# A triangular inversion of 62 small operations goes from VectorE's queue to GpSimd's, with an earlier turn

## What is computed

```python
logits = einsum('bhqd,bhkd->bhqk', q, k) * scale        # 16 heads of 8
probs = softmax(logits + causal_mask)
L = eye(s) - tril(probs, -1)
rhs = diagonal(probs)[..., None] * v
A = solve_triangular(L, rhs, lower=True)
x = x + ga * (A.transpose(0, 2, 1, 3).reshape(b, s, HID) @ Wd.T + bd)
```

## Time and profile before

| | us |
|---|---|
| median of 3 runs | 2507.65 (2505.02 to 2507.76) |
| the profiled execution | 2516.91 |
| its span, first to last instruction | 2515.2 |
| PE busy | 1845.2 (73%) |
| DVE busy | 1649.4 (66%), 3581 instructions |
| ACT busy | 548.0 (22%) |
| POOL busy | 466.2 (19%), 170 instructions |
| PE's granted clock, mean | 0.66 of full speed |

### The profile page before, as it was taken

One profiled execution on the slowest core, in us unless ns is written; L12 is line 12 of the kernel. 1 busy time (PEld: TensorE's weight loads), 2 busy tenths in 40 slices (PEclk: granted clock), 3 DMA queues, 4 the chain that ended last, 5 costly groups with the idle time before them and its releaser, 6 DMA issues.

```text
span 2515.2 us, 47927 instructions
## 1 busy us (share of the span) xinstructions
PE 1845.2 (73%) x20840; PEld 1331.0 (53%) x20840; DVE 1649.4 (66%) x3581; ACT 548.0 (22%) x787; POOL 466.2 (19%) x170
## 2 busy tenths in 40 slices
PE   1566436667677777777876976887888888888869
PEld 1343324444445444444543654666676767675759
DVE  6564367778866877678678547575656666657574
ACT  1100111222222323333333431111112120202010
POOL 9000011111110101001001100313131404040313
PEclk8666555555555556556557656696969696868687
DMA  3042942222111221012021120000000000000000
GB/s 118 2 99 64 151 96 50 50 50 50 46 36 26 49 50 44 8 49 44 8 44 43 40 73 1 1 5 1 5 1 5 1 5 1 5 1 5 1 5 5
DMA packets 130210, 83.87 MB, mean 33 GB/s; under 512 B 100690, under 2 KB 118100, under 8 KB 125524
## 3 DMA queue, kind: packets, MB, share of 16 engines
q1 hardware_dynamic: 130004, 80.85, 14.5%
HBM read 31.54 MB, written 49.28 MB: 32 GB/s over the span
## 4 chain that ended last, share of the span: by engine, by line
PE 44%; DVE 36%; issue 12%; POOL 2%; SPq 2%; DMA 2%; ACT 1%; DVEq 0%; POOLq 0%; ACTq 0%
PE pb L967 11%; DVE mraw L1159 8%; DVE zb L1207 6%; DVE tb L1202 6%; PE pb L975 5%; PE pb L954 4%; PE pb L850 3%; PE pb L801 2%; PE pb L762 2%; PE pb L870 2%; PE pb L880 1%; POOL cst L537 1%; DVE iv L1270 1%; DVE h L1247 1%; PE pb L946 1%
## 5 line engine op out<-in xcount | busy, mean ns | idle before, releaser
L1159 DVE TENSOR_REDUCE mraw<-pb 128x2 f32<-128x1024 f32 (+3 forms) x304 | 354.3, 1165 | 167.5 <-PE pb L806 123.2
L967 PE MATMUL pb<-r,hoty 128*128 128x64 f32 x2048 | 339.7, 348 | 75.4 <-DVE su L1335 45.3
L563 POOL TENSOR_TENSOR r<-hotx,wbd 128x2048 f32<-128x2048 f32 x32 | 248.7, 7771 | 753.8 <-DVE hotx L1322 753.8
L967 PEld LDWEIGHTS pb<-r,hoty 128*128 128x128 f32 x2048 | 336.5, 262 | 79.6 <-DVE su L1335 46.6
L801 PE MATMUL pb<-kall,qa 48*128 48x512 bf16 (+3 forms) x768 | 166.8, 473 | 244.9 <-DVE mraw L1159 193.2
L616 ACT ACTIVATE et<-pb 128x1024 f32<-128x1024 f32 x224 | 229.0, 1024 | 310.5 <-PE pb L817 309.3
L1202 DVE TENSOR_TENSOR tb<-cst,zb 128x31 f32<-128x31 f32 (+15 forms) x496 | 194.2, 392 | 65.8 <-POOL cst L537 53.2
L1207 DVE TENSOR_TENSOR zb<-zb,tb 128x31 f32<-128x31 f32 (+15 forms) x496 | 201.0, 405 | 13.5
L850 PE MATMUL pb<-et,a_all 128*9 128x128 f32 x3584 | 204.7, 368 | 1.7 <-ACT et L616 1.2
L1335 DVE TENSOR_TENSOR su<-su,pb 128x512 f32<-128x512 f32 x128 | 87.2, 686 | 176.1 <-PE pb L967 176.1
L801 PEld LDWEIGHTS pb<-kall,qa 48*128 48x128 bf16 x768 | 38.0, 110 | 306.7 <-DVE mraw L1159 243.7
(11 more groups left out here) (174 smaller groups left out, 2443.8 us busy)
## 6 DMA issues: line engine op xcount, KB each, us to landing
ed_d<-ed SPq DMA_DIRECT2D x32, 1024.0 KB, 4.6
cst<-ed_d SPq DMA_DIRECT2D x128, 64.0 KB, 5.1
qs_d<-qkp SPq DMA_DIRECT2D x48, 128.0 KB, 2.2
ks_d<-qkp SPq DMA_DIRECT2D x48, 128.0 KB, 2.3
qa<-qs_d SPq DMA_DIRECT2D x64, 96.0 KB, 2.6
kall<-ks_d SPq DMA_DIRECT2D x8, 672.0 KB, 21.2
xin<-L_attn_hidden_states SPq DMA_DIRECT2D x4, 512.0 KB
out<-xs SPq DMA_DIRECT2D x8, 256.0 KB, 2.2
```

The costliest lines, as they stand in the source:

```text
L563: nc.gpsimd.tensor_tensor(r4[:, n_ % 2, :, :, :], hotx[:, n_ % 2, :, :].unsqueeze(2).broadcast_to([P, NT, P // NT, NCH]), wbd[:, t, :, :]. ...
L967: last = mm(spread_w(q)[:, j].rearrange("p g c -> p (g c)"), hoty[:, n % 2, at, :], r4[:, n % 2, at, :, :].rearrange("p g c -> p (g c)"), ...
L1159: V.reduce_max(mraw[:, bb, :, g0:g0 + count, c0 // 512], pb[0][:, :].rearrange("p (e n) -> p e n", e=2)[:, :, 0:count * w].rearrange("p e ...
```

## The change

The 62 operations of an inversion leave DVE's queue for POOL's. There inversion s - 1 is cut in three around the masks of step s: 15 pairs of operations (blocks 0 to 2) or 2(2i - 1) pairs before mask (s, 0), three pairs between the masks, and the rest behind mask (s, 1). That makes 10, 14, 18, 22 and 26 pairs ahead of the masks for blocks 3 to 7. The last inversion stands behind all steps. DVE's plan keeps its begin and its turn, with one quota of 4 for all blocks from 3 on, so that the turn is 15 slots behind the begin: the begins of ss = 8 and 9 move to slots 150 and 170, and the solve groups of ss = 7 to 14 begin at slots 147, 167, 187, 211, 235, 263, 291 and 323. The turn waits for POOL's semaphore `inv_done`, in DVE's queue in front of the maxima of that slot. Behind the list the turn of the last inversion stands between two pairs of gates.

```diff
--- before.py
+++ after.py
@@ -108,7 +108,7 @@
             "e_lg", "exp_done", "av_done", "ed_masked", "ed_st0", "ed_st1", "x_ld0", "x_ld1",
             "r_done", "rT_sb", "rn_ps", "r_evac",
 
-            "rd_ready", "rdb_ready", "xb_ready", "zb_ready", "pool_link", "rn_ready", "z_ready", "px_done", "acur", "acc_done", "rr_ready",
+            "rd_ready", "rdb_ready", "xb_ready", "inv_done", "pool_link", "rn_ready", "z_ready", "px_done", "acur", "acc_done", "rr_ready",
 
             "xa_ld", "xr_ld", "tab_ld",
             "ac_ready", "at_ps", "at_sb", "y_ps", "h2_ready", "var2", "sd2", "h2T_ps", "h2T_sb", "gu_ps", "sg", "act",
@@ -362,7 +362,7 @@
                 room = first[ss + 1] + len(chunks_of(ss + 1)) - at
                 quota = -(-NOPS // room)
             else:
-                quota = 3 if block_of(ss + 1) > 3 else 4
+                quota = 4
             left = NOPS
             while left:
                 inv_at[at] = (ss, min(quota, left))
@@ -522,7 +522,7 @@
                 if ss:
                     g.wait_ge(s["z_ready"], ss)
                 lk(nc.gpsimd.memset(zb[:, :, :], 0.0))
-                nc.gpsimd.memset(zb[:, :, :].rearrange("p k i -> p (k i)")[:, 0:NB * NB:NB + 1], 1.0).then_inc(s["zb_ready"], 1)
+                lk(nc.gpsimd.memset(zb[:, :, :].rearrange("p k i -> p (k i)")[:, 0:NB * NB:NB + 1], 1.0))
 
             def mask(s_, bb):
                 wait_alone(g, "exp_done", chunk(s_, bb, 1) + 1, "passed_pool")
@@ -535,6 +535,21 @@
                 g.wait_ge(s["rdb_ready"], ss + 1)
                 g.wait_ge(s[x_ld[par]], 16 * 2 * NC * (ss // 2 + 1))
                 nc.gpsimd.tensor_tensor(xb[:, par, :, :], xb[:, par, :, :], rdb[:, :].unsqueeze(1).broadcast_to([P, NB, NB]), ALU.mult).then_inc(s["xb_ready"], 1)
+                g.wait_ge(s["xb_ready"], ss + 1)
+
+            def inverse(ss):
+
+                par = ss % 2
+                for j in range(NB - 1):
+                    w, u = NB - 1 - j, j + 1
+                    lk(nc.gpsimd.tensor_tensor(tb[:, 0:u, 0:w], xb[:, par, j:j + 1, u:].broadcast_to([P, u, w]),
+                                               zb[:, 0:u, j:j + 1].broadcast_to([P, u, w]), ALU.mult))
+                    total = nc.gpsimd.tensor_tensor(zb[:, 0:u, u:], zb[:, 0:u, u:], tb[:, 0:u, 0:w], ALU.add)
+                    if j < NB - 2:
+                        lk(total)
+                    else:
+                        total.then_inc(s["inv_done"], 1)
+                    yield
 
             def right_side(ss):
                 i, pr, par = block_of(ss), ss % 2, ss % 2
@@ -548,12 +563,26 @@
                 g.wait_ge(s["rd_ready"], ss + 1)
                 nc.gpsimd.tensor_tensor(to, to, rdn[:, par, :].rearrange("p (b h) -> p b h", b=2).unsqueeze(3).broadcast_to([P, 2, H, HD]), ALU.mult).then_inc(s["rn_ready"], 1)
 
+            def steps_of(work, count):
+                for _ in range(count):
+                    next(work, None)
+
             for s_ in range(STEPS):
-                mask(s_, 0)
-                mask(s_, 1)
+                if s_:
+                    i = block_of(s_)
+                    work = inverse(s_ - 1)
+                    steps_of(work, 15 if i <= 2 else (2 * i - 1) * 2)
+                    mask(s_, 0)
+                    steps_of(work, 3)
+                    mask(s_, 1)
+                    run(work)
+                else:
+                    mask(s_, 0)
+                    mask(s_, 1)
                 clear_inverse(s_)
                 scaled(s_)
                 right_side(s_)
+            run(inverse(STEPS - 1))
             for i in range(NI):
                 for t in range(B):
                     n_ = B * i + t
@@ -1191,25 +1220,8 @@
                 v.wait_ge(s["dve"], n[0])
                 v.sem_inc(s["rdb_ready"], 1)
 
-            def inverse(ss):
-
-                par = ss % 2
-                v.wait_ge(s["zb_ready"], ss + 1)
-                v.wait_ge(s["xb_ready"], ss + 1)
-                for j in range(NB - 1):
-                    w, u = NB - 1 - j, j + 1
-                    v.wait_ge(s["dve"], n[0])
-                    V.tensor_tensor(tb[:, 0:u, 0:w], xb[:, par, j:j + 1, u:].broadcast_to([P, u, w]),
-                                    zb[:, 0:u, j:j + 1].broadcast_to([P, u, w]), ALU.mult).then_inc(s["dve"], 1)
-                    n[0] += 1
-                    yield
-                    v.wait_ge(s["dve"], n[0])
-                    V.tensor_tensor(zb[:, 0:u, u:], zb[:, 0:u, u:], tb[:, 0:u, 0:w], ALU.add).then_inc(s["dve"], 1)
-                    n[0] += 1
-                    yield
-
             def turn_inverse(ss):
-                v.wait_ge(s["dve"], n[0])
+                v.wait_ge(s["inv_done"], ss + 1)
                 if ss:
                     v.wait_ge(s["px_done"], 4 * ss)
                 V.transpose(vt[:, :, :].rearrange("p m i -> p i m"), zb[:, :, :].rearrange("p k i -> p i k")).then_inc(s["z_ready"], 1)
@@ -1250,8 +1262,8 @@
                 lk(V.tensor_tensor(h2[:, :, :], h2[:, :, :], mod[:, :, 4, :], ALU.mult))
                 V.tensor_tensor(h2[:, :, :], h2[:, :, :], mod[:, :, 3, :], ALU.add).then_inc(s["h2_ready"], 1)
 
-            def gates(i):
-                for c in range(4):
+            def gates(i, cs=range(4)):
+                for c in cs:
                     v.wait_ge(s["sg"], 4 * i + c + 1)
                     V.tensor_tensor(hid[:, c, :, :].rearrange("p b n -> p (b n)"), sg[:, c % 2, :], pair(c)[:, 512:1024], ALU.mult).then_inc(s["act"], 1)
 
@@ -1343,19 +1355,13 @@
             nothing = iter(())
             for k in prologue:
                 max_job(k, nothing)
-            work = nothing
             for g_ in range(LAST):
-                if g_ in begin_at:
-                    work = inverse(begin_at[g_])
-
                 def some(g_=g_):
                     if g_ in begin_at:
                         begin_inverse(begin_at[g_])
                     if g_ in inv_at:
                         ss, count = inv_at[g_]
-                        for _ in range(count):
-                            next(work)
-                            yield
+                        yield
                         if inv_at.get(g_ + 1, (None, 0))[0] != ss:
                             turn_inverse(ss)
                 for k in jobs_at[2 * g_]:
@@ -1373,9 +1379,9 @@
             begin_inverse(STEPS - 1)
             attention_out(0)
             normed(0)
-            run(inverse(STEPS - 1))
+            gates(0, (0, 1))
             turn_inverse(STEPS - 1)
-            gates(0)
+            gates(0, (2, 3))
             next_rows(STEPS - 1, 1)
             keys_left = best_keys(0)
             next(keys_left)
```

## The result

The changed kernel takes 2549.56 us (median of 4, 2546.59 to 2554.18) against 2507.7 for the kernel before in the same measurement: ratio 1.0162, interval 1.0132 to 1.0192. Forecast were 2496 us. The profiled execution took 2548.56 us around a span of 2546.8, so the two profiled spans differ by 31.6 us. The medians differ by 41.9, since the profiled execution of the kernel before was 9.3 us above its median; what follows accounts for the 31.6.

The account below looks back on a forecast made before the run. The inversion's two operations held 24.3% of the attention stage's chain, with VectorE the bound early and TensorE close behind later. Terms -3 + 14 - 47 + 19 + 1 + 4 = -12 us took 2507.65 to 2496 us; range 2436 to 2562.

Parts of the forecast that it names:

- Three regimes: Attention stage: VectorE bounds inversions 0 to 3, TensorE is about as busy in 7 to 11, no maxima are left in 14.
- What one inversion costs on POOL: 62 operations on POOL, priced from operations of 256 and 1024 elements: 34 us, bounds 31 and 50 us.
- The link: Between an operation on POOL and its linked successor: 0.08 us from end to start.
- Steps 0 to 4: First five steps: 44.8 us each from begin to turn on POOL, what lies behind the turn unchanged; -3 us.
- Step 5: 18 pairs wait for slot 105's exponentials, which a mask of step 6 needs: 64 us against the window's 50.4, +13.7 us.
- Steps 6 to 13: Turn 15 slots behind the begin instead of 20, solve groups spread out, POOL's path 46.8 us in late steps: -47 us.
- The price of a plain slot behind the turn: Each of the five plain slots that now fall behind the turn, with no solve group or inversion: 2.6 us.
- Step 14: Window 32.6 becomes 44.8 us (+12); TensorE's last sums wait for a late mask, chunks done behind the groups (+7): +19 us.
- Step 15: Last inversion: window 39.65 us against 40.6 on POOL, +1 us.
- The port: VectorE operations with two SBUF operands can each wait for a POOL operation: +4 us in all, bounds 0 and 60.
- C: Rival: POOL's inversion dearer through the multiplication's operand with 128-byte steps, kernel slower, 2535 or 2575 us; chance 0.33.
- A: Rival: VectorE's relief is worth more, plain slots outside POOL's windows cost 2.0 us, about 2445 us; chance 0.20.

## Why the prediction was wrong, point by point

**What bounds the kernel.** Three regimes, with VectorE the bound in the first: right. It is why a dearer engine has no cover there.

**What one inversion costs on POOL, 34 us.** The first step that failed. The 62 operations with their links took 36.7 us: in step 0 from 330.08 to 371.15, less the two masks' 4.4 with their gaps. The timeline of POOL at its start, in step 2:

```profile
462.05 0.29 POOL L545 TENSOR_TENSOR tb<-cst,zb 128x60 f32<-128x60 f32 x1
462.42 0.29 POOL L547 TENSOR_TENSOR zb<-zb,tb 128x60 f32<-128x60 f32 x1
462.79 0.34 POOL L545 TENSOR_TENSOR tb<-cst,zb 128x87 f32<-128x87 f32 x1
463.20 0.34 POOL L547 TENSOR_TENSOR zb<-zb,tb 128x87 f32<-128x87 f32 x1
```

The price per element was too high (L545: 0.254 us at 31 and 0.643 at 256 elements, so 1.73 ns) and the fixed part far too low (0.20 us instead of 0.056): an operation of 87 elements took 0.34 us, not 0.25. A line through 256 and 1024 elements says little about 31, and I had named this extrapolation and added only 0.02 us for it. The link, 0.08 us, was right.

**Steps 0 to 4, -3 us: measured +19.** The path was put at 44.8 us and is 47.6 to 48.1. Five times 3.1 is 15 of the 22 us; the rest is 1.1 us a step between L524 and the next L537 (81.1 us before, 86.7 after, for the five), which the prediction had called unchanged. Where these inversions are VectorE's, this sum ranges from 75 to 86 us from trace to trace, so whether the rest is more than spread stays open. The run with only 0 to 4 on POOL shows that the loss is these steps' own.

**Step 5, +13.7: measured +15.3**, and taken away by 22 pairs ahead of the mask (103.6 to 87.6 us, and 106.2 to 90.5). Right.

**Steps 6 to 13, -47: measured -25.** The second step that failed, and the one with the most in it: the earlier turn and the slots that it puts behind the turn. The prediction had it as part of the gain, above all in steps 7 and 8. The eight steps from L537(6) to L537(14), in us, for every trace with 20 or 15 slots throughout and whole inversions (the places of the masks differ in two of them):

| | turn 20 slots behind from block 4 on | 15 slots behind |
|---|---|---|
| on VectorE | 697.6, 697.1 | 714.9 |
| on POOL | 643.8, 644.3, 649.0 | 672.5, 671.7, 666.0, 667.9 |

Moving the inversion alone brings 49 to 54 us, more than the 47 of the forecast. The earlier turn takes 17 to 29 us of it back, and it takes 17 where nothing is on POOL. So its cost can't be put down to POOL's path alone, and no run divides the 17 to 29 between that path, which the windows of 47.8 us show, and the plan. Why the earlier turn costs the kernel before 17 us is open.

In the prediction's own terms: the stretch between turn and next L537 was priced at 18.7 us for three groups and two plain slots (ss = 7, 8) and at 35 for step 10's nine slots. Measured were 22.8, 23.8 and 41.2, and 22.2, 23.7 and 41.1 in the kernel before with the earlier turn, so POOL has no part in it. With 2.5 us more in 11 to 13 that is 18 of the 22 us. The windows of 10 to 13 were 1 us longer each than the 46.8 forecast, step 7's window some 4 and step 6 2 us; against that step 9 was 3 us shorter, and the terms listed for step 8 add up to 69.3, not 72.8.

The price of a plain slot behind the turn, 2.6 us, was about right: 3.2 us in slots 242 to 246, 2.8 in 270 to 274, 2.4 in 298 to 306 of the changed kernel, by the starts of the exponentials. Only beside POOL's inversion is a slot cheaper: the exponentials of slots 274 and 287,

```profile
1326.62 1.02 ACT L645 ACTIVATE et<-pb 128x1024 f32<-128x1024 f32 x1 [0.26 <-PE pb L846]
1351.60 1.02 ACT L645 ACTIVATE ed<-pb 128x1024 f32<-128x1024 f32 x1 [0.91 <-PE pb L846]
```

are (1351.60 - 1326.62)/13 = 1.92 us a slot. So in step 13 fifteen slots passed in 34 us while POOL needed 48, and VectorE stood at the turn for the difference. The turns of ss = 4, 5, 13 and 14 on VectorE, with the wait ahead of each:

```profile
632.32 1.98 DVE L1227 STREAM_TRANSPOSE vt<-zb 128x1024 f32<-128x1024 f32 x1 [7.83 <-POOL zb L547]
714.52 2.01 DVE L1227 STREAM_TRANSPOSE vt<-zb 128x1024 f32<-128x1024 f32 x1 [24.79 <-POOL zb L547]
1374.20 2.01 DVE L1227 STREAM_TRANSPOSE vt<-zb 128x1024 f32<-128x1024 f32 x1 [13.47 <-POOL zb L547]
1473.40 2.05 DVE L1227 STREAM_TRANSPOSE vt<-zb 128x1024 f32<-128x1024 f32 x1 [45.86 <-POOL zb L547]
```

In ss = 10 to 12 the wait at the turn is only 0.8 to 2.9 us. There POOL's path shows in TensorE's waits for the masks and in VectorE's for TensorE behind them.

**Step 14, +19: measured +22**, by a reason half wrong. POOL's longer path (32.6 to 47.7 us, +15) is there. So is the hole on TensorE before the mask's sums, 23.6 us where near 19 were forecast, but it costs nothing of its own: with 9 pairs ahead the step took as long. The remaining 6.5 us lie between turn and next begin, where the last groups and chunks now come one after the other (12 exponentials against 7), as the forecast had said.

**Step 15, +1: measured +3** to the end of the kernel. Its window alone grew by 4.9 us, to 44.5; the inversion took 38.0 us instead of 34. **The port, +4**: the operations concerned are dearer. Groups by line, the second sum of each step's maxima, before and after:

```profile
L1178 DVE TENSOR_TENSOR esub<-ldg,mx 128x16 f32<-128x16 f32 x32 | 7.8, 243 | 1.1
```

```profile
L1207 DVE TENSOR_TENSOR esub<-ldg,mx 128x16 f32<-128x16 f32 x32 | 15.3, 480 | 1.1
```

Over all lines named there the busy time rose from 54 to 70 us, inside the bounds of 0 to 60 for what is added; how much of the 16 us is on the path was not measured apart. The same lengthening is what rows 7 and 8 show. The trace agrees with the rule that the prediction took from the Trainium skill, "SBUF — State Buffer", section "Who interferes with whom".

**The rivals.** C, POOL dearer and the kernel slower, came true by its sign and its condition (more than 35 us), not by its mechanism: the product with its 128-byte steps took 0.643 us at 256 elements, less than the sum (0.732). The rule of the Trainium skill ("GPSIMD Engine Reference", section "Performance pitfalls for Q7 kernels") asks for an inner step of at most 8 bytes; here the 128 bytes lie between rows and the step within a row is nothing, so the rule doesn't cover this operand, and the rival had no ground in it. What made POOL dearer was the fixed part of small operations. A put the relief above the forecast. That holds for the move alone, but not for its price of a slot outside POOL's windows (2.0 us; measured 2.4 to 3.2). The range, 2436 to 2562, held the result because it was wide; the chances put too much on faster.

## What to carry to other kernels

An operation moved to another engine is free only as long as what waits for it stands later in its queue than the operation's path is long: work out that path in us, and put beside it what the other engines have left to do there after the relief. Here moving inversions 6 to 13 brings 49 to 54 us, 2% of the kernel, if the plan is left alone, and costs where the inversion is the serial chain (steps 0 to 4, 14 and 15). And change one thing at a time: the earlier turn that came with the move took back a third to a half of its gain, and costs by itself too. When a ratio is better than the steps that were changed explain, look at the stages that weren't. For chains of small dependent operations the fixed cost sets the price; take it from an operation of that size, or widen the range by it.

## What the runs showed that I had not expected

The kernel before is sensitive to its quota: four operations a slot instead of three, with no work added, cost 25 us (ratio 1.0098). That three operations a slot fill VectorE's gaps and four overfill them is a guess, not tried apart. The expert stage took 17 to 21 us less in five kernels in which nothing of it was changed. And two fifths of POOL's operation are fixed cost at these sizes: of 0.52 us mean duration (267.1 + 250.0 us for the page's two groups of 496) some 0.20 don't depend on the elements, against 0.17 us by the same reckoning on VectorE, where in most cases 31 elements take 0.19 to 0.22 us and 256 take 0.42.
